# More places for probabilities, narrower masks and new orders in an eight-layer attention and feed-forward kernel

## The reference, cut to what matters

```python
x = x + attn_a(layernorm(x))     # causal, 16 heads of 16, over 1024 positions, with biases
x = x + ffn(layernorm(x))
x = x + attn_b(layernorm(x))     # sliding: each query sees the last 64 keys, the first 63 given
x = x + ffn(layernorm(x))

# attn_a
w = einsum('bhqd,bhkd->bhqk', q, k) / 4
w = softmax(w * mask - (1 - mask) * 1e6)
a = einsum('bhqk,bhkd->bhqd', w, v);  return a @ Wp + bp
# attn_b
scores = einsum('blhd,blwhd->blwh', q, k_win) * 16 ** -0.5
out = einsum('blwh,blwhd->blhd', softmax(scores, axis=2), v_win);  return out @ Wo.T
# ffn, weights are integers / 127
return (silu(x @ wg.T) * (x @ wu.T)) @ wd.T
```

## Time and profile before

| | |
|---|---|
| time, median of 3 runs | 1326.31 us (1325.27 to 1327.34) |
| profiled execution | 1328.82 us, its span 1327.1 us |
| mean granted clock of PE | 0.992 |
| PE busy | 1233.5 us, 93% |
| DVE busy | 860.1 us, 65% |
| ACT busy | 775.9 us, 58% |
| POOL busy | 417.8 us, 31% |

### The profile page before, as it was taken

One profiled execution on the slowest core, in us unless ns is written; L12 is line 12 of the kernel. 1 busy time (PEld: TensorE's weight loads), 2 busy tenths in 40 slices (PEclk: granted clock), 3 DMA queues, 4 the chain that ended last, 5 costly groups with the idle time before them and its releaser, 6 DMA issues.

```text
span 1327.1 us, 29244 instructions
## 1 busy us (share of the span) xinstructions
PE 1233.5 (93%) x11648; PEld 789.5 (59%) x11648; DVE 860.1 (65%) x1544; ACT 775.9 (58%) x1125; POOL 417.8 (31%) x406
## 2 busy tenths in 40 slices
PE   5999989998999999989999999999999999999988
PEld 5433458776853337866784333886687433488666
DVE  5888726556589845555659883555557988356562
ACT  4546765565654674657465567555655566755662
POOL 6612533213341213311344122441235212342132
PEclk9999999999999999999999999999999999999999
DMA  7600402634350031344343030143435203016330
GB/s 243 190 27 26 161 18 84 171 104 159 86 141 26 23 116 65 99 136 133 118 130 106 2 120 19 64 140 104 138 104 166 70 11 119 27 62 178 94 105 33
DMA packets 108967, 130.00 MB, mean 98 GB/s; under 512 B 29632, under 2 KB 89088, under 8 KB 107904
## 3 DMA queue, kind: packets, MB, share of 16 engines
q1 hardware_dynamic: 108832, 128.11, 31.9%
HBM read 46.21 MB, written 11.61 MB: 44 GB/s over the span
## 4 chain that ended last, share of the span: by engine, by line
PE 64%; ACT 10%; DVE 10%; issue 5%; SPq 5%; POOL 3%; DMA 2%; POOLq 0%; ACTq 0%; DVEq 0%
PE ring L1498 10%; PE ring L1470 9%; PE ring L1448 7%; PE ring L1538 6%; PE ring L1539 6%; DVE peak L1028 6%; ACT probs_causal L1224 6%; SPq L1743 4%; PE ring L1553 4%; PE ring L1558 3%; PE ring L1395 3%; PE ring L1361 2%; PE ring L1362 2%; PE ring L1363 2%; PE ring L1294 2%
## 5 line engine op out<-in xcount | busy, mean ns | idle before, releaser
L1028 DVE TENSOR_REDUCE peak<-ring 128x1 f32<-128x768 f32 (+8 forms) x416 | 405.6, 1012 | 83.9 <-PE ring L1395 64.5
L1224 ACT ACTIVATE probs_causal<-ring 128x1024 f32<-128x1024 f32 (+1 forms) x320 | 289.5, 938 | 174.7 <-PE ring L1470 153.2
L1470 PE MATMUL ring<-q_st,k_st 98*128 98x512 bf16 (+6 forms) x1408 | 242.4, 283 | 12.7 <-DMA q_st<-peak_b 3.4
L1448 PE MATMUL ring<-k_st,q_st 96*128 96x512 bf16 (+3 forms) x768 | 179.0, 328 | 14.8 <-DVE peak L1028 6.0
L1470 PEld LDWEIGHTS ring<-q_st,k_st 98*128 98x128 bf16 (+1 forms) x1408 | 101.8, 98 | 145.5 <-DVE peak L1028 41.0
L918 POOL TENSOR_SCALAR_AFFINE_SELECT probs_causal<-probs_causal 128x512 f32<-128x512 f32 x128 | 82.7, 648 | 306.5 <-ACT probs_causal L1224 306.3
L924 POOL TENSOR_TENSOR onf<-onf,o_hi 128x512 fp32r<-128x512 f32 x64 | 82.7, 1294 | 304.4 <-ACT o_hi L1244 304.4
L930 POOL TENSOR_TENSOR h_lo<-hid,h_hi 128x512 fp32r<-128x512 f32 x96 | 122.2, 1286 | 157.0 <-ACT h_hi L1277 156.4
L1498 PE MATMUL ring<-probs_causal,V 128*32 128x512 f32 (+3 forms) x1536 | 163.5, 501 | 4.0 <-POOL probs_causal L918 3.2
L1538 PE MATMUL ring<-xt_hi,w_gu_sb 128*128 128x512 f32 x384 | 152.1, 396 | 5.9 <-DVE xt_lo L962 5.2
L1539 PE MATMUL ring<-xt_lo,w_gu_sb 128*128 128x512 f32 x384 | 150.1, 391 | 0.0
(11 more groups left out here) (130 smaller groups left out, 2105.4 us busy)
## 6 DMA issues: line engine op xcount, KB each, us to landing
q_st<-q_part SPq DMA_DIRECT2D x192, 128.0 KB, 2.4
w_gu_sb<-img_gu SPq DMA_DIRECT2D x56, 384.0 KB, 4.5
k_st<-k_part SPq DMA_DIRECT2D x96, 144.0 KB, 2.6
k_st<-k_part SPq DMA_DIRECT2D x96, 128.0 KB, 2.4
w_qkv<-img_qkv SPq DMA_DIRECT2D x7, 1536.0 KB, 6.6
on_hi<-o_hi SPq DMA_DIRECT2D x64, 128.0 KB, 2.7
on_lo<-onf SPq DMA_DIRECT2D x64, 128.0 KB, 2.9
y<-X SPq DMA_DIRECT2D x8, 512.0 KB, 2.9
```

What stands on the lines that cost most here:

```text
L1028: dve.tensor_reduce(dst, scores, AX.X, ALU.max).then_inc(a_max, 1)
L1224: act.activation(block[0:rows, n % slots, h:h + heads, 0:w], heads_of(flat_of(a, e), unit, w)[0:rows], ACT.Exp).then_inc(exp_done, 1)
L1448: pe.matmul(psum[:, per * n + c:per * n + c + d], q, keys[0:SP_ROWS, head, W + c:W + c + d], start=(per * n % 512 == 0), stop=False, skip_ ...
L1470: last = pe.matmul(psum[0:rows, per * n:per * n + w], keys[:, head, first_key:first_key + rows], queries[:, head, q0 - HALF * hf:q1 - HALF ...
```

## The change

Three things are changed. First, the attention's second half (groups 4 to 7) gets three places for probabilities in causal layers and six in sliding ones; the added ones lie where `q_part` and part of `k_part` stood. `slot_of` and `slot_before` say which place a key tile takes and which V must be done before. The first exponentials of group 4 that find no V before them wait for the stacks (`stack_in`), and Silu of the first two gates, whose buffer lies there too, for the last V. In the plan the B of a tile also needs the first V of the group whose place it takes, and G0 the last V. DVE waits for its own peak_lo before it writes `peak_h` again. Second, the mask of a sliding A unit is added to the outer thirds of its 96 columns only, 4 heads x 2 x 32 columns. The middle third holds keys that every query of the 32 sees. The planner's cost of PE for such a unit goes from 0.75 to 0.58. Third, `LIKES` has new numbers for causal layers 2, 4, 6 and for sliding layers; layer 0 keeps its numbers, and the last layer has an entry of its own with the same numbers as the other sliding ones.

```diff
 LIKES = (
-    dict(turn=-0.43, ahead0=-0.31, ahead1=0.83, lead0=1.56, lead1=1.46, late=0.46, Q=-0.18, q=0.52, S=-3.7,
...
+    dict(turn=-0.5, ahead0=0.59, ahead1=0.09, lead0=1.7, lead1=1.28, late=-0.81, Q=-0.88, q=-0.77, S=-2.27,
...
-    dict(turn=2.37, ahead0=-1.15, ahead1=0.56, lead0=0.86, lead1=1.56, late=-2.79, Q=1.05, q=5, S=-1.31, E=-1.22,
...
+    dict(turn=3.33, ahead0=4.38, ahead1=1.74, lead0=3.58, lead1=1.94, late=2.31, Q=0.3, q=0.4, S=-0.05, E=3.75,
...
 def running(counts):
...
         self.chunks = 2 if self.causal else 3
-        self.slots = 2 if self.causal else 4
+        self.slots, self.more_slots = (2, 3) if self.causal else (4, 6)
         self.lns = [0, 1, 2, 3]
         self.tail = range(12 if self.final else 6)
-        self.us, self.program, self.banks, self.fill = self.order(LIKES[2 if self.opening else 0 if self.causal else 1])
+        self.us, self.program, self.banks, self.fill = self.order(LIKES[2 if self.opening else 3 if self.final else 0 if self.causal else 1])
 
...
         return self.v_base[sg] + j - self.keys[sg // 4][0]
+
+    def slot_of(self, sg, j):
+
+        n = self.v_index(sg, j)
+        if sg < 4:
+            return n % self.slots
+        return (n - self.v_base[4]) % self.more_slots
+
+    def slot_before(self, sg, j):
+
+        n = self.v_index(sg, j)
+        if sg < 4:
+            return n - self.slots if n >= self.slots else None
+        m = n - self.v_base[4]
+        if m >= self.more_slots:
+            return n - self.more_slots
+        return n - self.slots if m < self.slots else None
 
...
             if not self.causal:
-                return [("PE", 0.75, 0.2), ("DVE", 0.16 + 0.00104 * 2 * w, 0.05)]
+                return [("PE", 0.58, 0.2), ("DVE", 0.16 + 0.00104 * 2 * w, 0.05)]
             return [("PE", 0.055 * heads + 0.00043 * w, 0.2), ("DVE", 0.16 + 0.00104 * w, 0.05)]
...
             n = self.v_index(sg, self.b_units[sg // 4][k][0])
-            m = n - self.slots
-            older = [(("V",) + self.key_tiles[m], 0)] if m >= 0 else [] if self.opening or n >= self.slots // 2 else [(("j", 11), 1)]
+            m = self.slot_before(sg, self.b_units[sg // 4][k][0])
+            if m is not None:
+                older = [(("V",) + self.key_tiles[m], 0)]
+            elif sg >= 4:
+                older = [(("S", 1, 1, 5), 0)]
+            else:
+                older = [] if self.opening or n >= self.slots // 2 else [(("j", 11), 1)]
             if self.opening and n < self.slots:
                 older = older + [(("U", "bias"), 1), (("U", "kpre"), 0)]
-            return [[(("T", sg), 2), (("E", sg % 4 // 2), 0)], older, []][step]
+            begun = [(("V", self.key_tiles[m][0], self.keys[self.key_tiles[m][0] // 4][0]), 0)] if m is not None else []
+            return [[(("T", sg), 2), (("E", sg % 4 // 2), 0)] + begun, older, []][step]
         if kind == "V":
...
             else:
-                gate = [(("S", 1, 1, 5), 0)] if own else []
+                gate = [(("V",) + self.key_tiles[-1], 0)] if own else []
             return [turned, gate][step]
...
         r_p = region(33536)
-        probs = [at("probs_causal", r_p, [P, 2, HG, HALF], F32), at("probs_sliding", r_p, [P, 4, HG, HALF // 2], F32)]
+        probs = [at("probs_causal", r_p, [P, 3, HG, HALF], F32), at("probs_sliding", r_p, [P, 6, HG, HALF // 2], F32)]
         gate = [at("gate0", r_p + 16384, [P, 2, HALF], F32), at("gate1", r_p, [P, 2, HALF], F32)]
...
...
                         pool.wait_ge(exp_done, B_BASE[a] + plan.b_base[sg] + k + 1)
-                        block = probs[0][:, plan.v_index(sg, j) % 2, :, 0:P]
+                        block = probs[0][:, plan.slot_of(sg, j), :, 0:P]
                         pool.affine_select(out=block, in_=block, compare_op=ALU.is_ge, fill=0.0, base=0,
...
                         dve.wait_ge(a_max, A_BASE[a] + plan.a_base[sg + 1])
+                        if n:
+                            dve.wait_ge(peak_lo, n)
                         dve.tensor_copy(peak_h[:], peak[:, sg % 2, 0, :]).then_inc(peak_cut, 1)
...
                         act.wait_ge(b_ready, B_BASE[a] + plan.b_base[sg] + k + 1)
-                        block, slots = slots_of(a)
-                        if n >= slots:
-                            act.wait_ge(pv_done, V_BASE[a] + n - slots + 1)
+                        block, older = probs[a % 2], plan.slot_before(sg, j)
+                        if older is not None:
+                            act.wait_ge(pv_done, V_BASE[a] + older + 1)
+                        elif sg >= 4:
+
+                            for q in range(2):
+                                act.wait_ge(stack_in[q][1], 192 * (a + 1))
                         elif a == 0:
 
                             act.wait_ge(s_bias, 2)
                             act.wait_ge(s_kpre, 5)
                             act.wait_ge(s_ones, 32)
-                        elif n < slots // 2:
+                        elif n < plan.slots // 2:
 
                             act.wait_ge(h_lo_done, 12 * a)
                         w, rows = plan.b_width(hf, j), plan.key_rows(hf, j)
-                        act.activation(block[0:rows, n % slots, h:h + heads, 0:w],
+                        act.activation(block[0:rows, plan.slot_of(sg, j), h:h + heads, 0:w],
                                        heads_of(flat_of(a, e), unit, w)[0:rows], ACT.Exp).then_inc(exp_done, 1)
...
                                 act.wait_ge(stack_in[p][1], 192 * (a + 1))
+                            act.wait_ge(pv_done, V_BASE[a + 1])
                         elif kind == "g" and k < M_HID + 2:
...
                     for b in range(4):
-                        dst = psum[32 * b:32 * b + 32, t, 0:HG * REACH].rearrange("p (h c) -> p h c", c=REACH)
-                        window = mask_a[1][:, 32 * b:32 * b + REACH]
+                        dst = psum[32 * b:32 * b + 32, t, 0:HG * REACH]
+                        dst = dst.rearrange("p (h s c) -> p h s c", h=HG, s=3)[:, :, 0:3:2, :]
+                        ends = mask_a[1][:, 32 * b:32 * b + REACH].rearrange("p (s c) -> p s c", s=3)[:, 0:3:2, :]
                         last = pe.matmul(dst, ident_b[:, 32 * b:32 * b + 32],
-                                         window[:, None, :].to_broadcast([P, HG, REACH]),
-                                         start=False, stop=True, skip_group_check=True)
+                                         ends[:, None, :, :].to_broadcast([P, HG, 2, 32]), start=False, stop=True,
+                                         skip_group_check=True)
                 last.then_inc(a_ready, 1)
...
                 n = plan.v_index(sg, j)
-                block, slots = slots_of(a)
+                block = probs[a % 2]
                 if plan.causal and j >= 4 * hf:
...
                                      V[0:rows, j, HG * g + h, :, :].rearrange("p d o -> p (d o)"),
-                                     block[0:rows, n % slots, h, 0:q1 - q0],
+                                     block[0:rows, plan.slot_of(sg, j), h, 0:q1 - q0],
                                      start=opens, stop=closes, skip_group_check=True)
```

25 lines of the change are left out of this document (14 added, 11 removed).

## The result

| | before | after |
|---|---|---|
| time, median | 1325.79 us (4 runs, 1324.45 to 1327.34) | 1342.67 us (4 runs: 1337.59, 1337.61, 1347.73, 1347.94) |
| profiled execution, span | 1328.82, 1327.1 us | 1337.61, 1335.7 us |
| mean granted clock of it | 0.992 | 0.991 |

Ratio 1.013, 95% interval 1.0101 to 1.0158: **17 us slower (13 to 21), where 11 us faster was forecast**, and outside the range. The profiled execution is one of the two short ones, 8.6 us of span longer than before; the long ones had a clock of 0.985 and 0.986.

What follows compares the result with a forecast made beforehand. PE, 93% busy, was taken to bound the kernel, with waits for helpers left. Sliding layers -10.0, causal -4.5, layer 0 +3.3 sum to -11.2 us: 1315.1 us from the median of 1326.31, range 1304 to 1327.

Steps and rivals of the forecast that it cites:

- Causal layers, forecast -4.5: Layers 2, 4, 6: shorter tail less costs on PE, ACT and DVE, -1.5 us a layer, -4.5 in three.
- The tail: Causal layers behind V(7,7): G0 follows at once, W starts earlier; 25.0 us instead of 29.6, -4.6 a layer.
- DVE gets Q(0,1) and Q(1,1) ... I take 1.2: Causal layers: four DVE operations of 0.7 us move deeper into a stretch 85% busy; between 0 and 2.8, +1.2 taken.
- ACT's share, taken as 1.3: End of causal attention: 4.0 us of added ACT work, less 2.7 for exponentials now ahead of T7, +1.3 a layer.
- The table switch: ACT in causal layers: 1.41 us from load to next work by the trace; the skill's 2.66 would give 1318.8.
- Sliding layers, forecast -10.0: Layers 1, 3, 5, 7: new order and narrower masks bring V(3,4) earlier, -2.5 us a layer, -10.0 in four.
- waits -2.0: Sliding attention: maxima two groups ahead remove three PE waits, 3.45 us in layer 3; 2.0 taken, bounds 0 and 3.45.
- The chain from V(3,4) to O0: Sliding layers: copy, sums, reciprocal, product, split, packing take 15.1 us, and the layer's end follows this chain.
- The masks' price: Sliding score units: eight masks of 256 columns take 0.22 us, not 0.33; 0.11 less each, 1.6 counted before V(3,4).
- Layer 0, forecast +3.3: Layer 0: the plan's wait for a group's V puts 38 fillers for 25, 2.9 us, and delays B7; +3.3.
- The helpers' queues set the pace: Rival: work moved into full ACT and DVE queues counts in full, sliding layers gain nothing; +12.6, 1338.9 us; chance 0.12.
- Low clock: Tails after the wait for W: PE some microseconds at 1.2 GHz, none or all seven with other fillers; -4.5 to +6.

Runs made afterwards that it cites:

- e3: Kernel before with only causal layers 2, 4 and 6 as in the changed kernel (new order, three places), masks full width: ratio 1.0084 to before, 1338.14 us.
- e10: Changed kernel with GpSimd's bias addition to the residual done for a quarter of the tokens in layers 2, 4, 6 (output differs): 1.0048 to before, 1333.47 us.
- e14: Changed kernel with GpSimd's addition to the residual as eight instructions of one token tile each, nothing left out: ratio 1.0055 to before, 1334.83 us.
- e5: Kernel before with layers 2, 4, 6 changed only from the first B of group 4 on (new weights, three places): ratio 1.0033 to before.
- e2: Kernel before with only sliding layers 1, 3, 5, 7 as in the changed kernel (masks, six places, new order): ratio 1.003 to before, 1330.68 us.
- e1: Kernel before with the outer-third masks alone, all orders and places as before: ratio 0.9993 to before, 1326.91 us.
- e8: Kernel before with the third place in layer 0, without the rule that a B waits for its group's first V: ratio 0.9988 to before.
- e9: The changed kernel itself run once more, nothing altered: ratio 1.0108 to before, four executions from 1336.52 to 1343.35 us.
- e7: Kernel before with only the third place in the second half of layers 2, 4, 6, weights as before: ratio 0.9987 to before.

## Why the prediction was wrong

- **Causal layers, forecast -4.5, measured +8.8 in the trace and +11 as a part (e3).** The tail was right: forecast 25.0 us, measured 24.2, and G0 and O1 stand as said. The failed step is "DVE gets Q(0,1) and Q(1,1) ... I take 1.2": it priced the moved work by its own length, and put at nothing what the new first half does to the engines beside it. GpSimd's addition now meets VectorE's cast and holds it up. That is 2.1 to 2.3 us of wait a layer, and 0.6 to 1.5 more where the clock falls behind it: up to B(4,0) the layers lose 5.2, 3.7 and 4.3 us, not 1.2. Where the cast isn't held (e10) they lose 1.4, 1.2 and 0.5, which is about the 1.2 that was counted. Taken out, it gives 7 us (e10), and cut into pieces it gives 6 (e14). The criterion of the prediction, a causal stretch up to V(7,7) 4.6 us longer, was passed: 165.4 to 174.5 in layer 2.
- **ACT's share, taken as 1.3** with the third place at -0.3, was too low where the attention ends. With L2's 0.9 the sum had 1.9 us for the second half up to V(7,7); it is 3.9 at full clock, 3.2 of it ahead of T7. PE waits 1.97 us at L2 and 0.88 at O0. With the old first half (e5) the stretch from T7 to V(7,7) grows by 4.2, part of it by a clock of 0.94, and the whole is 0.33% slower. The prediction's own row showed ACT at 11.87 of 12.3 us; the slack it set against it lay in front of the loads, not behind.
- **The table switch.** From load to next work it is 1.41 us in the trace after too (507.52 to 508.93). The Trainium skill ("ScalarE: Activation LUTs", "What ACT_TABLE_LOAD costs") states 2.66 us for every switch. The traces here don't bear that out; the loss lies elsewhere.
- **Sliding layers, forecast -10.0; the trace has -4.8, e2 times them as +0.3%.** The step that failed is "waits -2.0". The waits for peaks did go, and others came: 1.06 us at the first A for V's copy, 1.36 at O0 (0.84 before), shorter ones for maxima. Before V(3,4) they sum to 3.9 us a layer, 3.2 before the change. The chain from V(3,4) to O0 (forecast 15.1, measured 14.9 to 16.6) was right, but not that the layer's end follows it: V(3,4) comes 1.2 us later and the layers are 1.2 shorter, by what lies behind O0, for which the sum took nothing. Why that stretch is shorter, and why a part that is shorter in the trace isn't faster in ten executions (e2), stays open; in e2's trace the causal layers, with their tails at the low clock, are 2.8 us longer and take it all back. The masks' price was right, 0.11 us, their worth was not: V(3,4) comes 0.65 us earlier in e1's trace where 1.6 was counted.
- **Layer 0, forecast +3.3.** The mechanism was right and the size low: +4.6 in the trace, +0.6% as a part, and by e8 the rule alone. The fillers' 2.9 were right; the waits beside them, 1.5, were missing.
- **The rivals.** "The helpers' queues set the pace", 1338.9, was nearest in time and had 0.12. That it came near is partly luck: its mechanism is only half of it, a full ACT, yes, but VectorE was not full, it was blocked.
- **Low clock.** The range named -4.5 to +6 for it. In the traces of the changed kernel the dips are mostly in the first half of causal layers (two of three layers, all three in e3 and e9), where they fall on Q's matmuls. In e10 they stand at the attention's end, in e2 in the causal tails, three times of three each. What places them is not explained.

## What to carry to other kernels

A reordering is priced by what the moved work releases late, as much as by its own length: follow each moved instruction to the store, and from it to the next big instruction that must wait for it, and ask what runs beside that one in its new place. Where VectorE has short SBUF work on PE's path, a long GpSimd instruction beside it is worth cutting into pieces: here that gave 6 us of 1341. Work taken off a PE that is 93% busy need not be worth its length, here less than 4 us of 7, as long as PE's next operand comes from a chain of helpers. A rule that delays the planner's choice can be a pure cost, as in layer 0; in e7's second half it was none.

## What the runs showed of the hardware

A VectorE instruction from SBUF to SBUF stands still while one GpSimd instruction that reads SBUF runs. A cast of 0.17 us took 2.29 to 2.48 and ended 0.03 to 0.04 us behind a tensor_tensor in three layers, 1.16 beside another in the trace of before, and 0.52 beside a mask (affine_select). A subtraction of two SBUF tiles took 0.63 instead of 0.17 (e14). Beside GpSimd's memset (395.48 to 396.43 in the changed kernel's trace), which only writes, the same subtraction took its usual 0.18. Maxima that read PSUM are not delayed.

The Trainium skill says so, "SBUF — State Buffer", "Who interferes with whom": the two engines share a pair of ports, a cast in a two-port mode takes it, and so does, against a GpSimd instruction that reads SBUF, an instruction with two SBUF inputs; whoever is first holds it for the whole instruction, and reductions never contend. The traces agree in who waits for whom, and e14 in that it is held for one instruction at a time; the ports themselves no trace shows.

Executions of one kernel differ by up to 10 us, and the mean granted clock goes with it: of its 25 runs beside e1, the kernel before took 1321.84 to 1324.90 us in the five at 0.996, and 1331.93 in the one at 0.989.
